# A two-layer block with routed experts: the last expert slot's rows by a permutation product, gathers one slot sooner, and place products ahead of half a key/value unit

## The reference

```python
x = x + tanh(g_xattn[0]) * xattn0(layernorm(x), ctx)   # 16 heads of 16
x = x + tanh(g_ffn[0]) * ffn0(layernorm(x))            # 8 experts, one per token
x = x + tanh(g_xattn[1]) * xattn1(layernorm(x), ctx)   # rms-normed queries and keys
x = x + tanh(g_ffn[1]) * ffn1(layernorm(x))            # self attention, then 16 experts, 6 per token
```

```python
route = sigmoid(t @ router_w); max_ind = argmax(route, 1)
out = sum over e of where(max_ind == e, (silu(t @ gate_w[e]) * (t @ up_w[e])) @ down_w[e], 0)
out = out * max(route, 1)
```

## Time and profile before

| | |
|---|---|
| median of 3 runs | 761.36 us (760.95 to 764.85) |
| the profiled execution | 763.18 us, its span 761.5 us |
| PE busy | 728.8 us, 96% of the span |
| DVE, ACT, POOL busy | 455.1 (60%), 374.2 (49%), 297.0 (39%) |
| chain that ended last | PE 81%, DVE 7%, ACT 6%, POOL 2%, DMA 2%, issue 1% |
| TensorE clock granted | full in 39 of 40 slices, 7 tenths in the 11th |

### The profile page before, as it was taken

One profiled execution on the slowest core, in us unless ns is written; L12 is line 12 of the kernel. 1 busy time (PEld: TensorE's weight loads), 2 busy tenths in 40 slices (PEclk: granted clock), 3 DMA queues, 4 the chain that ended last, 5 costly groups with the idle time before them and its releaser, 6 DMA issues.

```text
span 761.5 us, 14062 instructions
## 1 busy us (share of the span) xinstructions
PE 728.8 (96%) x4683; PEld 611.3 (80%) x4684; DVE 455.1 (60%) x823; ACT 374.2 (49%) x876; POOL 297.0 (39%) x376
## 2 busy tenths in 40 slices
PE   7999989999889989999999999999999999999998
PEld 6887657887567767898899988998778888888886
DVE  6888587554687854345444554355555665665665
ACT  4888236664377754445445454445442323323323
POOL 3233265664655656422232123212324434434430
PEclk9999999999799999999999999999999999999999
DMA  8980121111300011010110101200004343343321
GB/s 286 418 329 2 28 83 36 55 41 35 118 2 1 2 36 36 22 35 22 36 55 21 34 21 46 72 1 22 22 25 129 114 121 100 121 116 99 122 95 56
DMA packets 24745, 57.40 MB, mean 75 GB/s; under 512 B 3568, under 2 KB 13296, under 8 KB 23680
## 3 DMA queue, kind: packets, MB, share of 16 engines
q1 hardware_dynamic: 23936, 54.77, 22.0%
q0 software_dynamic: 768, 2.10, 0.9%
HBM read 50.76 MB, written 6.09 MB: 75 GB/s over the span
## 4 chain that ended last, share of the span: by engine, by line
PE 81%; DVE 7%; ACT 6%; POOL 2%; DMA 2%; issue 1%; DVEq 0%; SPq 0%; ACTq 0%; POOLq 0%
PE PS L351 16%; PE PS L353 16%; PE PS L352 16%; PE PS L1824 7%; PE PS L1482 4%; PE PS L465 3%; PE PS L500 2%; PE PS L509 2%; PE PS L471 2%; PE PS L1830 2%; PE PS L1467 2%; PE PS L1464 2%; PE PS L1461 2%; PE PS L522 1%; POOL Z L846 1%
## 5 line engine op out<-in xcount | busy, mean ns | idle before, releaser
L1250 ACT ACTIVATE hhh<-hh 128x512 fp32r<-128x512 f32 x50 | 31.6, 632 | 104.6 <-DVE hh L1276 94.7
L351 PE MATMUL PS<-tTh,wh 128*128 128x512 f32 x200 | 78.3, 392 | 0.8 <-DVE tTl L661 0.5
L353 PE MATMUL PS<-tTh,wl 128*128 128x512 f32 x200 | 77.9, 389 | 0.0
L352 PE MATMUL PS<-tTl,wh 128*128 128x512 f32 x200 | 77.8, 389 | 0.0
L661 DVE TENSOR_TENSOR hhl<-hh,hhh 128x512 fp32r<-128x512 f32 x50 | 52.3, 1047 | 35.4 <-ACT hhh L1250 35.4
L1342 POOL CAST wh<-wraw 128x512 fp32r<-128x512 f32 (+1 forms) x50 | 26.1, 523 | 109.9 <-PE PS L353 109.9
L2038 POOL CAST ah<-araw 128x512 fp32r<-128x512 f32 (+1 forms) x32 | 16.2, 506 | 134.6 <-PE PS L353 134.6
L1935 ACT ACTIVATE sm<-sm,nmx 128x128 f32<-128x128 f32 x128 | 49.7, 390 | 37.7 <-DVE nmx L1998 37.7
L661 DVE TENSOR_TENSOR oTl<-PS,oTh 128x512 fp32r<-128x512 f32 x32 | 22.1, 691 | 71.5 <-ACT oTh L1929 71.5
L1344 POOL TENSOR_TENSOR wl<-wraw,wh 128x512 fp32r<-128x512 f32 (+1 forms) x50 | 58.0, 1160 | 8.4 <-POOL wh L1342 7.9
L1531 POOL TENSOR_TENSOR wgl<-WE,wgh 128x512 fp32r<-128x512 f32 x28 | 46.9, 1696 | 26.4 <-ACT wgh L1577 25.8
(11 more groups left out here) (276 smaller groups left out, 1985.4 us busy)
## 6 DMA issues: line engine op xcount, KB each, us to landing
WE<-moe SPq DMA_DIRECT2D x8, 1536.0 KB, 18.1
wraw<-moe SPq DMA_DIRECT2D x25, 384.0 KB, 3.0
araw<-attn SPq DMA_DIRECT2D x16, 384.0 KB
cwb<-cw_d SPq DMA_DIRECT2D x20, 256.0 KB, 3.9
WX<-wx SPq DMA_DIRECT2D x4, 512.0 KB, 7.2
avraw<-attn_v SPq DMA_DIRECT2D x8, 256.0 KB
xs_d<-zeros SPq DMA_DIRECT2D x1, 1920.0 KB, 22.2
ys_d<-y_s SPq DMA_DIRECT2D x15, 128.0 KB, 1.7
```

Of the source, the lines that this page charges most:

```text
L351: nc.tensor.matmul(out, wh_, xh_, start=first, stop=False, **kw)
L352: nc.tensor.matmul(out, wh_, xl_, start=False, stop=False, **kw)
L353: return nc.tensor.matmul(out, wl_, xh_, start=False, stop=last, **kw)
L1250: nc.scalar.activation(hhh[half][:, :], hh[half][:, :], ACT.Copy).then_inc(s.hi_done, 1)
```

## The change

**The last slot.** Slot 14's rows are no longer stored to `ys_d`. Its part of `ys_d` is filled with zeros at the start, so a gather finds zeros for rows that lie in slot 14, and the gathers wait for the stores of slots 0 to 13 only. SP stores the places to DRAM (`pos_d`, 4-byte pieces) and broadcasts them to all partitions in two transfers; in slot 2 DVE compares them with the row numbers, which gives `last_perm`, the permutation of slot 14. After slot 14 PE makes eight products of it with `y_s[0]` (`last_product`). For tiles 0 to 3 PE adds the gathered rows in PSUM by a product with the identity (`gathered_rows`), and DVE adds the sum to x from there; for tiles 4 to 7 ACT copies the products to SBUF, and DVE adds these and the gathered rows in two additions. DVE adds tiles 0 and 1 before units 6 and 7, tiles 2 and 3 after them, tiles 4 and 5 in step -1, tiles 6 and 7 in step 0.

**The keys.** The units' keys are turned in another order (`TURNED`), four units around the last down product, two after the products; those of units 6 and 7 are turned in step -1 of the attention. The 15 fillers are left out, and of four others two stay.

**The place products.** PE runs two fillers before the last router product, and only half of unit 0 before the place products, with one filler between these. On DVE unit 0's work comes before the first low weights, and in slot 0 slot 1's low up weights come before unit 5's keys. The powers of the row norms are taken in other groups.

```diff
+LATE_KEYS = KEYS[B - 2:]
+TURNED = [4, 5, 0, 1, 2, 3]
+TURN_BANKS = [1, 3, 0, 2, 7, 6]
...
+        last_perm = rT[:, :, (B - CTX) * S:]
+        last_rows = gs2[:, :, :].rearrange("p a (k d) -> p (a k) d", d=D)
...
+                if L and b == 0:
+                    pe.wait_ge(Es.k1_ready, 2)
+                    pe.wait_ge(Es.last_read, 2)
...
-            pe.wait_ge(Es.kt_free, B)
-            fill(4, 7)
+            pe.wait_ge(Es.kt_free, len(TURNED))
+            fill(2, 7)
...
+                if n == -1:
+                    pe.wait_ge(Es.k1_ready, 2)
+                    for b in LATE_KEYS:
+                        rows_to_columns("KT", b, K1[:, b, :])
...
-                key_columns(act, MOST, B)
...
-                if n == -1:
-                    rest_of_rows()
+                if n in (-1, 0):
+                    rest_of_rows(EARLY + 2 * n + 2)
...
         def ffn_pe(pe):
             s = Es
+            fill(2, 0)
             pe.wait_ge(xs[0].act_free, reads_no[0]["F", B - 1])
...
-            nc.tensor.matmul(PS[:, 6, 0:P], ones[:, :], earlier[:, :], start=True, stop=True).then_inc(s.ids_done, 1)
+            nc.tensor.matmul(PS[:, 6, 0:P], ones[:, :], earlier[:, :], start=True, stop=True).then_inc(s.lg_done, 1)
...
-            keys_values(0)
-            fill(2, 0)
+            keys_values(0, (0,))
             pe.wait_ge(s.hot_done, 1)
...
             nc.tensor.matmul(pl, earlier[:, :], hot[:, 1:, :], start=True, stop=False)
+            fill(1, 0)
             pe.wait_ge(s.sums_done, 1)
             nc.tensor.matmul(pl, ones[:, :], sums_to[2][:, 3:, :], start=False, stop=True).then_inc(s.place_done, 1)
+            keys_values(0, (1,))
             keys_values(1)
...
+            def keys_back(k):
+                i, out = TURNED[k], PS[:, TURN_BANKS[k], :]
...
+            def last_product(b, signal=False):
+                if b in FIRST_OF_BANK:
+                    pe.wait_ge(s.kt_free, FIRST_OF_BANK.index(b) + 1)
+                m = nc.tensor.matmul(last_bank(b), last_perm[:, b // EARLY, b % EARLY * P:(b % EARLY + 1) * P], y_s[0][:, :], start=(b in FIRST_OF_BANK), stop=signal, skip_group_check=True)
...
+            def gathered_rows(b):
+                pe.wait_ge(s.gathered[b], 16)
+                if b >= FIRST:
+                    pe.wait_ge(s.place_read, b)
+                nc.tensor.matmul(last_bank(b), ident[:, :], FX[:, b, :], start=False, stop=True, skip_group_check=True).then_inc(s.last_done, 1)
             turn_hidden(SLOTS - 1)
+            keys_back(0)
+            keys_back(1)
             down(SLOTS - 1, (SLOTS - 1) % 2)
-
+            keys_back(2)
+            keys_back(3)
+            pe.wait_ge(s.perm_done, 2)
+            pe.wait_ge(s.y_ready, SLOTS)
+            for b in (0, 2, 1, 3):
+                last_product(b)
+            gathered_rows(0)
+            gathered_rows(1)
             for i in range(MOST, B):
                 keys_values(i)
-
-            for i in range(B):
-                if i == MOST:
-                    pe.wait_ge(s.kt_free, 3)
-                    fill(15, 2)
...
+            for b in range(EARLY, B):
+                last_product(b, b % 2 == 1)
+            keys_back(4)
+            keys_back(5)
+            gathered_rows(2)
+            gathered_rows(3)
...
-            key_columns(act, 0, MOST)
+            key_columns(act, 0, EARLY)
+            for k in range(2):
+                act.wait_ge(s.last_done, 3 + k)
+                nc.scalar.activation(gs2[:, k, :], PS[:, TURN_BANKS[2 + k], :], ACT.Copy).then_inc(s.last_read, 1)
+            key_columns(act, EARLY, len(TURNED))
...
-            dve.wait_ge(Es.gathered[b], 16)
-            ch.link(nc.vector.scalar_tensor_tensor(out=X[:, b, :], in0=FX[:, b, :], scalar=rmax[:, b:b + 1], in1=X[:, b, :], op0=ALU.mult, op1=ALU.add))
+            def add(src):
+                return nc.vector.scalar_tensor_tensor(out=X[:, b, :], in0=src, scalar=rmax[:, b:b + 1], in1=X[:, b, :], op0=ALU.mult, op1=ALU.add)
+            if b < EARLY:
+                dve.wait_ge(Es.last_done, b + 1 if b < FIRST else b + 3)
+                add(last_bank(b)).then_inc(Es.place_read, 1)
+                dve.wait_ge(Es.place_read, b + 2)
+            else:
+                dve.wait_ge(Es.last_read, 2)
+                ch.link(add(last_rows[:, b - EARLY, :]))
+                dve.wait_ge(Es.gathered[b], 16)
+                ch.link(add(FX[:, b, :]))
...
+            v.tensor_reduce(rows_after[:, :], earlier[:, :], AX.X, ALU.add)
...
                 if is_first(j):
-                    keys_values(4, MOST)
+                    keys_values(4, MOST - 1, False)
+                    low_ups(1, e)
+                    keys_values(MOST - 1, MOST)
                     output_rows(0, 0, 0)
                     low_columns(1, 1)
-                    low_ups(1, e)
...
+                if isinstance(j, int) and j == 2:
+                    dve.wait_ge(late_in, 64 + 16 * C)
+                    v.tensor_scalar(last_perm, last_perm, rows_after[:, :], float(SLOTS * P - 1), ALU.add, ALU.is_equal).then_inc(s.perm_done, 1)
...
+            keys_values(0, 1, False)
             low_gates(0, e)
-            keys_values(0, 1, False)
...
-                pool.wait_ge(s.y_out[par], 16 * ((SLOTS + 1 - par) // 2))
+                pool.wait_ge(s.y_out[par], 16 * ((SLOTS - par) // 2))
...
+            sp.wait_ge(s.pos_done, 1)
+            sp.dma_start(pos_d.rearrange("b p -> p b"), posf[:, :], allow_slow_non_contiguous=True).then_inc(late_in, 16)
+            sp.wait_ge(late_in, 64)
+            for c in range(C):
+                sp.dma_start(last_perm[:, c, :], pos_d[EARLY * c:EARLY * (c + 1), :].rearrange("b p -> (b p)").partition_broadcast(P)).then_inc(late_in, 16)
...
-            store(SLOTS - 1, (SLOTS - 1) % 2)
```

94 lines of the change are left out of this document (55 added, 39 removed).

## The result

| | before | changed |
|---|---|---|
| median, us | 761.94 (4 runs, 760.95 to 764.85) | 773.65 (4 runs, 769.44 to 775.53) |
| ratio | | 1.0146, 95% interval 1.0112 to 1.0181 |
| profiled execution, us (its span) | 763.18 (761.5) | 771.9 (770.2) |
| mean granted clock of it | 0.988 | 0.987 |

What follows compares the result with a forecast made beforehand. PE was taken as the bound, busy 96% of the span, with time to be had only in routing and passage. Routing -0.8 and passage +3.3 sum to +2.5; against the median of 761.36 that is 763.9, range 760.2 to 766.8.

Steps and rivals of the forecast that it cites:

- Routing, -0.8: Expert routing: reordered place products and DVE work bring the first expert's hidden rows 0.8 us sooner, bounds -1.5 and +0.5.
- the exchange of the low up weights with unit 5's keys fills DVE waits: Slot 0 on DVE: this reordering was given no separate cost, only included in the routing bounds of -1.5 and +0.5.
- The store, costed at 0: SP's store of positions in 4-byte pieces, with its wait and two broadcasts ahead of later slot loads: 0 us.
- the 12 us until slot 1's load: SP queue: some 12 us with nothing else queued cover the position store and broadcasts, so they cost 0.
- rival, at 0.03: Slow positions' store holds slot 1's load beyond 110, each us over the cover costing one; 765 or above, chance 0.03.
- Passage, +3.3: From experts to second attention: pass 1's probabilities are transposed at 226.9 against 223.55, 3.3 us later.
- Steps 3 and 5: Passage: ACT's queue delays first normed columns to 204.6; DVE's additions put tile 0's division 17.36 after the first softmax starts.
- step 1: Passage: gathers wait for slot 13, so POOL starts 3.2 us sooner, at 188.4; the second lands at 193.9.
- step 2: Passage, PE in order: last two key/value units wait behind the second gather, run 194.4 to 198.0; products end at 199.8.
- the slower rival: Clock falls during PE's wait for the gathers, losing 1.5 us or more on units and products; 766.4, chance 0.2.
- The rule weighed: PE transposes do not count as busy for the clock's monitor; by it the lost-clock rival's sum would hold.
- Any shift at that point lasts to the end: From pass 1 of the second attention PE is the bound, so a shift there lasts to the end.

Runs made afterwards that it cites:

- e1: Changed kernel without the position store and the two broadcasts that read it back; 768.12 us, 1.0099 of the kernel before.
- e4: Kernel before with the 1,024-piece position store alone added, read by nobody; 762.87 us, 1.0026 of the kernel before.
- e14: e2 with the broadcasts waiting until slot 0's up product is done; 766.52 us, 1.0075 of the kernel before.
- e2: Changed kernel with positions transposed and stored as 8 rows of 512 bytes, broadcasts kept; 768.39 us, 1.0102 of the kernel before.
- e5: e2 with Scalar's masked keys and Exp table ahead of the copies of the last slot's rows; 766.67 us, 1.0070 of the kernel before.
- e6: e2 with units 6 and 7 and the other four permutation products ahead of TensorE's wait for gathered rows; 769.48 us, 1.0102 of the kernel before.
- e13: Changed kernel with its 1,024-piece store kept and the two broadcasts left out; 768.17 us, 1.0075 of the kernel before.
- e9: The changed kernel once more, unaltered, beside the others on one chip; 770.90 us, 1.0125 of the kernel before.
- e10: Changed kernel with the place part undone, the last slot's part and its store kept; 775.06 us, 1.0155 of the kernel before.
- e3: Changed kernel with the 1,024-piece store moved behind slot 1's row store, broadcasts and comparison into slot 13; 770.31 us, 1.0121 of the kernel before.
- e11: e5 with the additions of sequences 4 to 7 one to a step, steps 0 to 3; 767.94 us, 1.0075 of the kernel before.
- e12: e11 with the place part undone, unit 6 ahead of the gathered rows, GpSimd's power after the fourth gather; 762.34 us, 0.9998 of the kernel before.
- e16: e12 with each late GpSimd power at the end of the step; 762.69 us, 1.0008 of the kernel before.

## Why the prediction was wrong, step by step

- **Routing, -0.8.** The gain at slot 0's hidden product is there but smaller, 0.3 at full clock (e1 against e4) and 0.5 at half (e14 against before); the 0.8 to 0.9 of e1 and e2 against the profile before is for the rest their clock, which is luck. The step that failed is "the exchange of the low up weights with unit 5's keys fills DVE waits": it put the read of the sixth unit behind a low part that ran beside GpSimd's, and the gain had turned into a loss at slot 1's columns (0.7 in e1 against e4, 0.4 in e14 against before). The two fillers took 0.73 in the changed kernel, and 1.22 where the routing began at half clock (e5, e6), not the 0.49 that I took.
- **The store, costed at 0.** This is the larger error: the step that failed is the cover that set its cost to 0. I named as cover the 12 us until slot 1's load, and as rival, at 0.03, one in which that load is late. The load came 0.9 later from the mark (107.61 less 85.62, against 107.84 less 86.72), and nothing waited for it. What stood was other traffic: the scatters stood for 5 us and Scalar for 4.6, in slot 0. The price was 3.1 in the profiles and 3.2, give or take 2.1, in the times. It takes the broadcasts too: the store without them cost 0 to 0.5% (e4, e13). How the two hold Scalar stays open. The Trainium skill, page "DMA: Bandwidth & Descriptors", Specifications, says that transfers under 512 bytes are read, changed and written back. That goes with the 11.6 us from issue to end of 4 KB, and with the eight rows of 512 bytes in e2, whose broadcasts start 1.3 us after the store's issue; it does not say that other queues stand meanwhile, which these runs show.
- **Passage, +3.3.** Measured +5.5, and the same in e1, e2, e9 and e10 (62.7 to 62.8), where the clock fell in the wait; +3.8 and +4.1 in e3 and e14, where it did not; +5.1 in e13. Steps 3 and 5, the Scalar queue and VectorE's additions, were right in mechanism: taking the queue off the path (e5) gave the first scores 1.8 to 2.1 us at the same clock, and the division came within 0.5 us of the working. Mis-sized were step 1 (gathers 2.65 sooner instead of 3.2, the second landing 5.75 later instead of 5.5) and above all step 2: units 6 and 7 at 5.14 instead of 3.6, because the clock fell in the wait; all told the fall cost 1.4 to 1.7. That is the slower rival, to which I gave 0.2 and 766.4; with it the passage is 5.8, close to what was measured.
- **The rule weighed** stays undecided. The clock fell where TensorE had transposes, eight small products and 2 us of idleness behind it; e6, with the same transposes and no idle time, kept it. But e3, e5 and e14 had the same transposes and 2.5 to 2.8 us of idleness, against 2.5 in the changed kernel, and kept it too. So neither the transposes nor the length of the wait decides it in these runs.
- **"Any shift at that point lasts to the end"** held within 0.9 us in the changed kernel, and failed for e11 and e12, where GpSimd set a later step.
- **The numbers.** Sum: 763.2 + 3.4 + 5.5 + 0.9 - 1.1 = 771.9. Two causes that I held for small or unlikely came together, the store and the clock in the wait, and I had drawn the range as if only one could. The store's 3.1 alone would have put the forecast at 767.0, just outside; the clock alone was inside, at 766.4.

## What to carry to other kernels

A store of single words is not priced by who waits for it alone; look at what shares the DMA engines while it ends. Here it cost 3 us with two broadcasts behind it and next to nothing without them. Put the words side by side first (one transpose and one copy here) or move it to where no engine needs a transfer. When a wait for a gather is put ahead of work, price the clock in that wait, and look at what stands behind it on every in-order engine: here Scalar's masked keys and table, which had been free. Compare two profiles only at the same clock in the same stretch: about half of what looked like the gain in routing was the clock. Gathers that start 2.65 us sooner were worth nothing in the end (e12, e16: level with before); that the products and the second additions they need cost as much is the likely reason, and was not measured apart.

## What the runs showed of the hardware

A store of 4 KB in 1,024 pieces is moved in under 2 us and is complete only 10 to 12 us after its issue (93.23 to 104.84; 93.17 to 103.61; 94.85 to 105.37). Meanwhile the scatters, in another queue, stand for some 5 us, and an instruction-queue packet comes 3 to 4.5 us later than without it (from the mark 19.5 in the changed kernel against 15.0 in e1; 19.0 in e4 against 16.0 before). With the broadcasts behind it Scalar was held 4.6 to 7.6 us, in three of three profiles, and had stood 0.9 to 2.0 us when they were issued; with the store alone it was not held, in two of two.

The same instructions at the same place run at full clock in one execution and at half in the next (88 to 92 us: 1.00 in the changed kernel, 0.50 in e6, with the same TensorE order there but for one transpose later; units 6 and 7 behind the same wait: 5.14 us in the changed kernel, 3.60 in e3 and e14), and the medians of a kernel contain both.
